# A four-stage transformer kernel on one core: the halves of the expert weights move in front of a weight split, and a norm's statistics move behind a residual add

## The chip, the core and the metric

The kernel runs on one core of a Trainium2 chip. The metric is the device time of one execution in microseconds (us); lower is better. TensorE (PE in the profile) multiplies matrices, with its weight loads as PEld; VectorE (DVE), ScalarE (ACT) and GpSimd (POOL) work on vectors, and SyncE (SP) issues the transfers. Each engine runs its own instruction list in the order in which it is written, and engines wait for each other by semaphores.

## The reference

Two transformer layers work on `x` (16 sequences of 64 tokens, 256 channels, float32). Each adds a gated cross attention and a gated feed-forward part. The part that matters here is the first layer's feed-forward, a mixture of 16 experts:

```python
probs = softmax(flat @ gate_w.T)
routing_weights, selected = top_k(probs, 4)
routing_weights = routing_weights / routing_weights.sum(-1)
comb = sum(one_hot(selected, 16) * routing_weights[..., None], axis=1)
for e in range(16):
    out_e = (silu(flat @ Wg[e]) * (flat @ Wu[e])) @ Wd[e]
    mixed = mixed + comb[:, e:e + 1] * out_e
shared = (silu(flat @ sWg) * (flat @ sWu)) @ sWd
return mixed + shared * sigmoid(flat @ shared_gate_w)
```

`flat` is the layer norm of `x`. Every expert is computed for every token, and the combined weight `comb` of token and expert scales its hidden values.

## The kernel before, in words

The 1024 tokens are worked on in four groups of 256 (`GROUPS`, two tiles of 128 rows each). There are four phases: A (cross attention of layer one), B (its experts), C (cross attention of layer two) and D (its feed-forward). Each phase runs over the four groups. The order of the work is written out by hand, once for each engine, in functions `pe_*`, `act_*`, `dve_*`, `pool_*` and `sp_*`; the last group of A and group 0 of B are interleaved in a merged stage (`pe_AB`, `act_AB`, `dve_AB`), and groups 1 to 3 of B are `pe_B`, `act_B`, `dve_B`. POOL has no merged function: it runs `pool_A` for all groups and then `pool_B` for all groups.

Float32 matmuls are made exact enough by splitting each operand into two halves: the upper half is a rounded copy (ACT, `nc.scalar.copy`), the lower half is what is left of it (a subtraction on DVE or POOL). `mm3` (L312) then multiplies upper by upper, upper by lower and lower by upper. So "halves" below always means such a pair.

One group of B, with k running over the 8 pairs of experts and the shared expert (`EC` = 8):

- `pe_B_gate_up` k makes gate and up of a pair in PSUM; ACT takes the tanh (`act_B_tanh`, L1090), DVE multiplies (`dve_B_gated`, L1169 and L1173), which gives h2.
- The router's logits become the combined weights on DVE. `pe_B_comb` (L971) turns them around with two transposes into 17 rows, `act_B_comb` (L1100) makes their upper half and `dve_B_comb` (L1229) their lower half.
- `pe_B_spread` k (L982) is one matmul with a selection matrix that spreads the two weights of a pair over the 128 hidden rows. The first one waits for both halves of the combined weights.
- `dve_B_weighted` k (L1179) multiplies h2 by the spread weights to h3; `act_B_upper` (L1105) and the loop of `pool_B` (L1304) make its halves, and `pe_B_down` k multiplies them with the down weights and sums over k in PSUM. It waits for both halves.
- Beside this, phase C's weights are prepared: `pe_B_join` r, for r from 0 to 3, multiplies two weight blocks into one PSUM bank (L644 for r of 0 and 1), `act_B_join` (L1117) and `dve_B_join` (L1185) make the halves of the product. Join r + 1 writes the same bank and so waits for the DVE's lower half of join r.

The order of PE in a group of B is: logits, gate/up 0, 1, 2, join 0, the transposes of the combined weights, gate/up 3, spread 0, spread 1, join 1, gate/up 4, down 0, and on. In the merged stage it is: gate/up 3, attention values, the transposes, gate/up 4, spread 0, spread 1, attention output (`pe_A_out`, L378 and at its end L382), down 0, spread 2, gate/up 5. Gate/up 5 writes the bank of the attention output and waits for the DVE's residual add (`dve_A_add`, L606).

The norm for the next group's `x` has three steps on three places: `front_stats` on DVE (L241, L245, L247) gives the variance, `front_pool` on POOL (L262) takes it to the power of -0.5, `front_norm` on DVE (L253) applies it; `front_pe` (L283) turns the result around for the matmuls much later in the group. On POOL the second step stands at the head of each group of B, and the change does not touch it:

```python
        def pool_B(pool, g):
            front_pool(pool, 5 + g)
            for k in range(EC + 1):
                n = rows_B(k)
                pool.wait_ge(*Bp["h_hi"].at(g, k + 1))
```

At the very start PE issues matmuls that only keep it going (`keep_warm`, L631).

Of the kernel before, what the change touches and what calls it, by code (L numbers as in the profile page):

```python
# [85 lines left out]
def build(nc, a):  # L86
    ctx = ExitStack()
    with ctx:
# [149 lines left out]
        def front_stats(dve, f, g):  # L238

            for t in range(TILES):  # L240
                nc.vector.bn_stats(stats[:, t, :], x[:, g * TILES + t, :]).then_inc(*front["stat"].up())  # L241
            for t in range(TILES):
                dve.wait_ge(*front["stat"].at(f, t + 1))
                dve.sem_inc(waited, 1)
                nc.vector.bn_aggr(mv[:, t, :], stats[:, t, :]).then_inc(*front["stat"].up())  # L245
            dve.wait_ge(*front["stat"].at(f, 4))
            nc.vector.tensor_scalar(ve, mv[:, :, 1], 1e-5, None, ALU.add).then_inc(*front["var_ready"].up())  # L247

        def front_norm(dve, f, g):

            dve.wait_ge(*front["rstd_ready"].at(f, 1))
            for t in range(TILES):
                nc.vector.tensor_scalar(xn[:, t, :], x[:, g * TILES + t, :], mv[:, t, 0:1], rstd[:, t:t + 1],  # L253
                                        ALU.subtract, ALU.mult).then_inc(*front["xn_ready"].up())
# [37 lines left out]
        def front_upper(act, f, to, hi=xT_hi):  # L292
            act.wait_ge(*front["xT_done"].at(f, 1))
            nc.scalar.copy(split_tokens(hi), ps[:, to, :]).then_inc(*front["hi_ready"].up())
# [620 lines left out]
        def rows_B(k):  # L915
            return P if k < EC else F
# [7 lines left out]
        def spread_of(k):  # L924
            return ps[:, (5, 2)[k % 2], 0:TG]

        def gate_B(g, k):
            bank = (6, 5, 4, 1, 0, 3, 1, 4, 3)[k] if g == 0 else (3, 4, 1)[k % 3]
            return ps[:, bank, 0:TG]
# [8 lines left out]
        def combT_B(g):  # L938
            return ps[0:E + 1, 6, TG:2 * TG]
# [145 lines left out]
        def act_B_tanh(act, g, k):  # L1085
            act.wait_ge(*Bp["gu_done"].at(g, k + 1))
            if k >= 3:
                act.wait_ge(*Bp["h1"].at(g, k - 2))
            n = rows_B(k)
            nc.scalar.activation(th[k % 3][0:n], gate_B(g, k)[0:n], ACT.Tanh,  # L1090
                                 scale=0.5).then_inc(*Bp["tanh_ready"].up())

        def act_B_router(act, g):
            act.wait_ge(*Bp["shifted"].at(g, 1))
            nc.scalar.activation(ex, ex, ACT.Exp).then_inc(*Bp["exp_ready"].up())
            nc.scalar.activation(sgate, lgs[:, :, E], ACT.Tanh, scale=0.5).then_inc(*Bp["gate_ready"].up())

        def act_B_comb(act, g):
            act.wait_ge(*Bp["combT_done"].at(g, 1))
            nc.scalar.copy(combT_hi, combT_B(g)).then_inc(*Bp["combT_hi"].up())  # L1100

        def act_B_upper(act, g, k):
            act.wait_ge(*Bp["h3"].at(g, k + 1))
            n = rows_B(k)
            nc.scalar.copy(h_hi[k % 3][0:n], h3[k % 3][0:n]).then_inc(*Bp["h_hi"].up())  # L1105

        def join_of(g, r):
            return (ps[:, 0, :] if g else joined[:, r]).rearrange("p (h n) -> p h n", h=2)

        def act_B_join(act, g, r):  # L1110
            if g:
                act.wait_ge(*Bp["join_done"].at(g, r + 1))
            elif r == 0:
                act.wait_ge(*A["x_done"].at(GROUPS, 0))
                act.wait_ge(joined_dve, 2)
            w = JOIN[r][0][:, bass.ds(g * HG + 2 * (r % 2), 2), :]
            nc.scalar.copy(w, join_of(g, r)).then_inc(*Bp["join_hi"].up())  # L1117
# [29 lines left out]
        def act_B(act, g):  # L1147
            act_B_tanh(act, g, 0)
            act_B_router(act, g)
            act_B_tanh(act, g, 1)  # L1150
            act_B_tanh(act, g, 2)
            act_B_join(act, g, 0)
            act_B_comb(act, g)
            act_B_upper(act, g, 0)
            for k in range(3, EC + 1):
                act_B_tanh(act, g, k)
                act_B_upper(act, g, k - 2)
                if k in (3, 5):
                    act_B_join(act, g, k // 2)
            front_upper(act, 5 + g, 0)  # L1160
            act_B_upper(act, g, EC - 1)
            act_B_upper(act, g, EC)
            act_B_join(act, g, 3)

        def dve_B_gated(dve, g, k):

            n = rows_B(k)
            dve.wait_ge(*Bp["tanh_ready"].at(g, k + 1))
            nc.vector.scalar_tensor_tensor(out=h1[k % 3][0:n], in0=th[k % 3][0:n], scalar=1.0,  # L1169
                                           in1=gate_B(g, k)[0:n], op0=ALU.add,  # L1170
                                           op1=ALU.mult).then_inc(*Bp["h1"].up())
            dve.wait_ge(*Bp["h1"].at(g, k + 1))
            nc.vector.tensor_tensor(h2[k % 3][0:n], h1[k % 3][0:n], up_B(g, k), ALU.mult).then_inc(*Bp["h2"].up())  # L1173

        def dve_B_weighted(dve, g, k):
            n = rows_B(k)
            dve.wait_ge(*Bp["h2"].at(g, k + 1))
            dve.wait_ge(*Bp["bc_done"].at(g, k + 1))
            nc.vector.tensor_tensor(h3[k % 3][0:n], h2[k % 3][0:n], spread_of(k)[0:n],  # L1179
                                    ALU.mult).then_inc(*Bp["h3"].up())  # L1180

        def dve_B_join(dve, g, r):
            dve.wait_ge(*Bp["join_hi"].at(g, r + 1))
            hi, lo = (w[:, bass.ds(g * HG + 2 * (r % 2), 2), :] for w in JOIN[r])
            nc.vector.tensor_tensor(lo, join_of(g, r),  # L1185
                                    hi.bitcast(F32), ALU.subtract).then_inc(*Bp["join_lo"].up())
# [40 lines left out]
        def dve_B_comb(dve, g):  # L1227
            dve.wait_ge(*Bp["combT_hi"].at(g, 1))
            nc.vector.tensor_tensor(combT_lo, combT_B(g), combT_hi.bitcast(F32),  # L1229
                                    ALU.subtract).then_inc(*Bp["combT_lo"].up())  # L1230
# [9 lines left out]
        def dve_AB(dve):  # L1240
            a, g = GROUPS - 1, 0
            dve_A_top(dve, a, 0)
            dve_A_top(dve, a, 1)
            dve_B_logits(dve, g)
            dve_A_lower(dve, a - 1)
            dve_A_sum(dve, a, 0)
            dve_A_sum(dve, a, 1)
            dve_B_choice(dve, g)
            dve_A_add(dve, a - 1)
            dve_B_weights(dve, g)  # L1250
            dve_B_gated(dve, g, 0)
            dve_B_gated(dve, g, 1)
            dve_B_gated(dve, g, 2)
            front_stats(dve, 5, 1)
            dve_A_lower(dve, a)
            dve_B_comb(dve, g)
            dve_B_weighted(dve, g, 0)
            dve_B_gated(dve, g, 3)
            dve_B_weighted(dve, g, 1)
            dve_B_gated(dve, g, 4)  # L1260
            dve_A_add(dve, a)
            front_norm(dve, 5, 1)
            for k in range(5, EC):
                dve_B_weighted(dve, g, k - 3)
                dve_B_gated(dve, g, k)
                dve_B_join(dve, g, k - 5)
            dve_B_weighted(dve, g, EC - 3)
            dve_B_gated(dve, g, EC)
            dve_B_weighted(dve, g, EC - 2)
            front_lower(dve, 5, 0)  # L1270
            dve_B_weighted(dve, g, EC - 1)
            dve_B_weighted(dve, g, EC)
            dve_B_join(dve, g, 3)
            dve_B_add(dve, g)

        def dve_B(dve, g):
            front_stats(dve, 5 + g, after(g))
            dve_B_logits(dve, g)
            dve_B_choice(dve, g)
            dve_B_weights(dve, g)  # L1280
            dve_B_gated(dve, g, 0)
            dve_B_gated(dve, g, 1)
            dve_B_gated(dve, g, 2)
            dve_B_join(dve, g, 0)
            dve_B_comb(dve, g)
            dve_B_weighted(dve, g, 0)
            front_norm(dve, 5 + g, after(g))
            for k in range(3, EC + 1):
                dve_B_weighted(dve, g, k - 2)
                dve_B_gated(dve, g, k)  # L1290
                if k in (3, 5):
                    dve_B_join(dve, g, k // 2)
            dve_B_weighted(dve, g, EC - 1)
            front_lower(dve, 5 + g, 0)
            dve_B_weighted(dve, g, EC)
            dve_B_join(dve, g, 3)
            dve_B_add(dve, g)
# [831 lines left out]
```

## Time and profile before

| | us |
|---|---|
| median of 3 runs | 404.07 |
| lowest, highest | 403.46, 405.74 |
| the profiled execution | 404.01 |
| its span on the core | 402.2 |
| PE busy | 374.7 (93%) |
| DVE busy | 312.0 (78%) |
| ACT busy | 194.0 (48%) |
| POOL busy | 168.9 (42%) |

The span runs from the first to the last instruction; what the profiled execution took beyond it (404.01 less 402.2) lies around it. Matmuls overlap, so a row of a matmul lasts longer than the distance to the next one: 0.28 us against about 0.12 us for 256 columns. Starts are therefore the better measure on PE. Experts and join work lie between 80 us and 191 us of the span: the merged stage up to 110 us, then groups 1, 2 and 3 of 27 us each.

### The profile page before, as it was taken

How to read it: one execution, taken by the hardware profiler on the slowest of the kernel's cores; microseconds unless marked ns; L12 is line 12 of the kernel's file. 1: busy time of each engine (PE TensorE's matmuls, PEld its weight loads, DVE VectorE, ACT ScalarE, POOL GpSimd, SP SyncE). 2: the span in 40 equal slices, each digit the busy share in tenths (PEclk: the TensorE clock that was granted, in tenths of full speed). 3: DMA queues.
4: the chain of work that ended last, by engine and by line, in shares of the span. 5: the costliest groups of instructions: out<-in, count | busy, mean ns of one | idle time of the engine just before them, and what ended most of it. 6: DMA issues, size and time to landing. Idle time of an engine off the chain costs nothing.

```text
span 402.2 us, 8995 instructions
## 1 busy us (share of the span) xinstructions
PE 374.7 (93%) x3586; PEld 351.7 (87%) x3594; DVE 312.0 (78%) x710; ACT 194.0 (48%) x401; POOL 168.9 (42%) x207
## 2 busy tenths in 40 slices
PE   0989999998999999999999999999999999999996
PEld 0777879887899999999999898999989999999996
DVE  3888878697786786775588988898899799965553
ACT  3577677742523333243356635554653556233332
POOL 4246646342303313123255545457424853632332
PEclk9999999999999999999999999999999999999999
DMA  7902102120000300300200010020001000000000
GB/s 219 337 13 78 57 30 80 34 102 2 0 2 0 133 2 1 132 0 10 75 0 2 6 63 2 2 67 3 2 0 56 3 0 2 2 10 19 27 28 27
DMA packets 7166, 16.33 MB, mean 41 GB/s; under 512 B 1218, under 2 KB 4803, under 8 KB 6740
## 3 DMA queue, kind: packets, MB, share of 16 engines
q1 hardware_dynamic: 7124, 15.75, 11.5%
q8 instruction: 28, 0.46, 0.5%
q14 instruction: 14, 0.11, 0.1%
HBM read 14.70 MB, written 1.05 MB: 39 GB/s over the span
## 4 chain that ended last, share of the span: by engine, by line
PE 60%; DVE 24%; ACT 8%; issue 4%; POOL 2%; DMA 1%; DVEq 0%
PE ps L312 37%; PE ps L1385 7%; DVE work L1656 4%; PE ps L414 2%; PE ps L378 2%; ACT work L1522 2%; DVE work L1173 2%; DVE work L1169 1%; ACT work L1500 1%; PE ps L1406 1%; DMA stage<-in_wA 1%; POOL workr L1304 1%; PE ps L982 1%; DVE workr L1613 1%; PE ps L425 1%
## 5 line engine op out<-in xcount | busy, mean ns | idle before, releaser
L1725 POOL TENSOR_SCALAR work<-work,lut_step,lut 128x344 f32<-128x344 int32 (+1 forms) x60 | 42.2, 715 | 53.6 <-DVE work L1641 52.0
L312 PE MATMUL ps<-wB_hi,workr 128*128 128x256 f32 x224 | 50.8, 293 | 3.0 <-POOL workr L1304 1.8
L312 PE MATMUL ps<-xT_hi,wB_hi 128*128 128x256 f32 x176 | 51.1, 290 | 0.3 <-DVE x L606 0.3
L312 PE MATMUL ps<-xT_lo,wB_hi 128*128 128x256 f32 x176 | 49.7, 282 | 0.0
L312 PE MATMUL ps<-xT_hi,wB_lo 128*128 128x256 f32 x176 | 49.7, 282 | 0.0
L1304 POOL TENSOR_TENSOR workr<-work,workr 128x256 fp32r<-128x256 f32 (+1 forms) x36 | 22.9, 636 | 62.3 <-ACT workr L1105 62.2
L312 PE MATMUL ps<-wN_hi,shared_r 128*128 128x256 f32 x256 | 47.8, 281 | 0.0
L1656 DVE COPY_PREDICATED work<-work 128x1376 f32<-128x1376 int32 (+5 forms) x36 | 42.1, 1168 | 2.2
L312 PEld LDWEIGHTS ps<-wB_hi,workr 128*128 128x128 f32 x224 | 38.2, 189 | 6.0 <-issue 3.3
L312 PEld LDWEIGHTS ps<-wN_hi,shared_r 128*128 128x128 f32 x256 | 40.2, 188 | 0.4 <-DVE shared_r L1618 0.3
L312 PE MATMUL ps<-xT_hi,wM_hi 128*128 128x256 f32 x128 | 36.6, 286 | 2.3 <-ACT work L1481 2.3
L312 PE MATMUL ps<-wN_lo,shared_r 128*128 128x256 f32 x128 | 35.6, 278 | 0.0
L312 PE MATMUL ps<-xT_lo,wM_hi 128*128 128x256 f32 x128 | 35.5, 277 | 0.0
L312 PE MATMUL ps<-xT_hi,wM_lo 128*128 128x256 f32 x128 | 35.5, 277 | 0.0
L312 PEld LDWEIGHTS ps<-xT_hi,wB_hi 128*128 128x128 f32 x176 | 33.5, 190 | 1.0 <-DVE x L606 0.5
L1090 ACT ACTIVATE work<-ps 128x256 f32<-128x256 f32 (+1 forms) x36 | 13.8, 384 | 41.7 <-PE ps L312 41.6
L312 PEld LDWEIGHTS ps<-xT_lo,wB_hi 128*128 128x128 f32 x176 | 33.5, 191 | 0.0
L312 PEld LDWEIGHTS ps<-xT_hi,wB_lo 128*128 128x128 f32 x176 | 33.5, 191 | 0.0
L1897 POOL TENSOR_TENSOR workr<-work,workr 128x256 fp32r<-128x256 f32 x24 | 19.5, 813 | 30.4 <-ACT workr L1844 30.2
L312 PE MATMUL ps<-wB_lo,workr 128*128 128x256 f32 x112 | 31.5, 281 | 0.0
L1385 PEld LDWEIGHTS ps<-stage,work 128*128 128x128 f32 x256 | 31.1, 192 | 0.4
L1385 PE MATMUL ps<-stage,work 128*128 128x64 f32 x256 | 30.3, 272 | 0.5
(220 smaller groups left out, 1072.7 us busy)
## 6 DMA issues: line engine op xcount, KB each, us to landing
stage<-in_wC SPq DMA_DIRECT2D x3, 1280.0 KB, 5.6
stage<-in_wB SPq DMA_DIRECT2D x4, 768.0 KB, 4.3
stage<-in_idx SPq DMA_DIRECT2D x4, 536.0 KB, 3.4
work<-in_wC SPq DMA_DIRECT2D x2, 640.0 KB, 7.7
stage<-in_wA SPq DMA_DIRECT2D x2, 512.0 KB, 5.6
out<-x SPq DMA_DIRECT2D x8, 128.0 KB, 1.8
x<-in_x SPq DMA_DIRECT2D x2, 256.0 KB, 4.6
x<-in_x SPq DMA_DIRECT2D x1, 512.0 KB, 9.7
```

The source lines that it names most:

```text
L312: last = nc.tensor.matmul(out, l, r, start=start and i == 0, stop=stop and i == 2)
L378: nc.tensor.matmul(ps[:, to, t * D:(t + 1) * D], l[:, c, tok], r[:, c, :], start=t == 0 and c == 0 and i == 0, stop=False, skip_group_chec ...
L414: last = nc.tensor.matmul(ps[:, p, k * S:(k + 1) * S], qx[r, k].rearrange("p h n -> p (h n)"), kT[r, k], start=k == 0, stop=False, skip_gr ...
L425: last = nc.tensor.matmul(o[:, :, lo:hi], ident_A, bc_last(neg_maxA[:, t, first:first + 8], hi - lo), start=False, stop=True, skip_group_c ...
L1090: nc.scalar.activation(th[k % 3][0:n], gate_B(g, k)[0:n], ACT.Tanh, scale=0.5).then_inc(*Bp["tanh_ready"].up())
L1173: nc.vector.tensor_tensor(h2[k % 3][0:n], h1[k % 3][0:n], up_B(g, k), ALU.mult).then_inc(*Bp["h2"].up())
L1304: nc.gpsimd.tensor_tensor(h_lo[k % 3][0:n], h3[k % 3][0:n], h_hi[k % 3][0:n].bitcast(F32), ALU.subtract).then_inc(*Bp["h_lo"].up())
L1385: last = nc.tensor.matmul(ps[:, 3 + s, k * S:(k + 1) * S], qt[:, 2 * s + jj, b].rearrange("p h n -> p (h n)"), ctx_g[:, b * S:(b + 1) * S] ...
L1522: nc.scalar.activation(lev[:, j, 0:n], bits[:, 0, 0:n], ACT.Identity, scale=lut_step[:, j:j + 1], bias=lut[:, 2 * j:2 * j + 1]).then_inc(* ...
L1656: nc.vector.copy_predicated(left, m, right).then_inc(*C["chosen"].up())
L1725: nc.gpsimd.tensor_scalar(lev[:, j, 0:n], bits[:, 0, 0:n], lut_step[:, j:j + 1], lut[:, 2 * j:2 * j + 1], ALU.mult, ALU.add).then_inc(*C[" ...
L1897: nc.gpsimd.tensor_tensor(fh_lo[i][0:n], fh3[k % 3][0:n], fh_hi[i][0:n].bitcast(F32), ALU.subtract).then_inc(*Dp["h_lo"].up())
```

## The change

In groups 1 to 3 of phase B the halves of the combined weights come before the halves of join 0, on ACT and on DVE. In the merged stage the DVE's statistics of the next norm go from in front of the lower halves of the attention output and of the combined weights to behind the residual add, and applying the norm goes from behind the add into the first round of the loop, behind join 0. ACT in the merged stage, PE and POOL keep their order.

```diff
 def act_B(act, g):
             act_B_router(act, g)
             act_B_tanh(act, g, 1)
             act_B_tanh(act, g, 2)
+            act_B_comb(act, g)
             act_B_join(act, g, 0)
-            act_B_comb(act, g)
             act_B_upper(act, g, 0)
 def dve_AB(dve):
             dve_B_gated(dve, g, 2)
-            front_stats(dve, 5, 1)
             dve_A_lower(dve, a)
             dve_B_comb(dve, g)
             dve_B_weighted(dve, g, 0)
             dve_B_gated(dve, g, 3)
             dve_B_weighted(dve, g, 1)
             dve_B_gated(dve, g, 4)
             dve_A_add(dve, a)
-            front_norm(dve, 5, 1)
+            front_stats(dve, 5, 1)
             for k in range(5, EC):
                 dve_B_weighted(dve, g, k - 3)
                 dve_B_gated(dve, g, k)
                 dve_B_join(dve, g, k - 5)
+                if k == 5:
+                    front_norm(dve, 5, 1)
 def dve_B(dve, g):
             dve_B_gated(dve, g, 2)
+            dve_B_comb(dve, g)
             dve_B_join(dve, g, 0)
-            dve_B_comb(dve, g)
             dve_B_weighted(dve, g, 0)
```

The DVE in the merged stage, before. The rows begin with the second half of gated 2; `L598` is the lower half of the attention output, `L1229` that of the combined weights, `L606` the residual add.

```order
L1173 TENSOR_TENSOR work<-work,ps 128x256
L241 BN_STATS stats<-x 128x6 x2
L245 BN_AGGR mv<-stats 128x2 x2
L247 TENSOR_SCALAR ve<-mv 128x2
L598 TENSOR_TENSOR workAr<-ps,workAr 128x2x4x64
L1229 TENSOR_TENSOR workr<-ps,workr 17x256
L1179 TENSOR_TENSOR work<-work,ps 128x256
```

And the same engine with the change, from `L598` on:

```order
L598 TENSOR_TENSOR workAr<-ps,workAr 128x2x4x64
L1229 TENSOR_TENSOR workr<-ps,workr 17x256
L1179 TENSOR_TENSOR work<-work,ps 128x256
L1169 SCALAR_TENSOR_TENSOR work<-work,ps 128x256
L1173 TENSOR_TENSOR work<-work,ps 128x256
L1179 TENSOR_TENSOR work<-work,ps 128x256
L1169 SCALAR_TENSOR_TENSOR work<-work,ps 128x256
L1173 TENSOR_TENSOR work<-work,ps 128x256
L606 SCALAR_TENSOR_TENSOR x<-ps,tg,x 128x512
L241 BN_STATS stats<-x 128x6 x2
L245 BN_AGGR mv<-stats 128x2 x2
L247 TENSOR_SCALAR ve<-mv 128x2
```

Five instructions of statistics now follow the add instead of preceding the two lower halves; nine instructions in front of them (two of weighting, four of gating, two lower halves, the add) moved ahead.

The DVE in groups 1 to 3, as one piece of the difference (join 0's lower half is `L1185`):

```order
 L1173 TENSOR_TENSOR work<-work,ps 128x256
+L1229 TENSOR_TENSOR workr<-ps,workr 17x256
 L1185 TENSOR_TENSOR wM_lo<-ps,wM_hi 128x512
-L1229 TENSOR_TENSOR workr<-ps,workr 17x256
 L1179 TENSOR_TENSOR work<-work,ps 128x256
```

The small subtraction passes the large one; the same happens to the two copies on ACT.

## Rows read from the trace of the kernel before

**Rows 1.** The page: TensorE's granted clock over the span in 40 slices.

```profile
PEclk9999999999999999999999999999999999999999
```

**Rows 2.** Who waited for whom: in total, times, longest, in us.

```profile
PE ps L982 <- DVE workr L1229: 3.0, 4, 1.2
...
PE ps L312 <- POOL workr L1304: 2.3, 8, 0.7
```

**Rows 3.** Timeline, merged stage: start, us, engine, line, operation, [idle before].

```profile
90.27 0.59 ACT L571 CAST workAr<-ps 128x512 fp32r<-128x512 f32 x1 [1.03 <-PE ps L528]
...
90.67 0.75 DVE L241 BATCH_NORM_STATS2 stats<-x 128x6 f32<-128x256 f32 x2
...
91.70 0.28 PE L312 MATMUL ps<-xT_hi,wB_lo 128*128 128x256 f32 x1
91.78 0.17 DVE L247 TENSOR_SCALAR ve<-mv 128x2 f32<-128x2 f32 x1
91.86 0.69 DVE L598 TENSOR_TENSOR workAr<-ps,workAr 128x512 fp32r<-128x512 f32 x1
92.03 0.70 POOL L262 TENSOR_TENSOR rstd<-ve,expo 128x2 f32<-128x2 f32 x1 [5.79 <-DVE ve L247]
92.57 0.41 DVE L1229 TENSOR_TENSOR workr<-ps,workr 17x256 fp32r<-17x256 f32 x1
93.13 0.47 PE L982 MATMUL ps<-workr 128*128 128x256 f32 x2 [1.15 <-DVE workr L1229]
```

**Rows 4.** Timeline, merged stage, from the halves of h3 to weighted 2.

```profile
94.54 0.64 POOL L1304 TENSOR_TENSOR workr<-work,workr 128x256 fp32r<-128x256 f32 x1 [1.81 <-ACT workr L1105]
...
94.86 0.40 PE L382 MATMUL ps<-workAr 128*128 128x512 f32 x1
...
95.33 0.36 PE L312 MATMUL ps<-wB_hi,workr 128*128 128x256 f32 x1
...
95.85 0.74 DVE L606 SCALAR_TENSOR_TENSOR x<-ps,tg,x 128x512 f32<-128x512 f32 x1
...
96.51 0.72 DVE L253 TENSOR_SCALAR xn<-x,mv,rstd 128x256 f32<-128x256 f32 x2
96.65 0.39 PE L312 MATMUL ps<-xT_hi,wB_hi 128*128 128x256 f32 x1 [0.26 <-DVE x L606]
...
97.15 0.41 DVE L1179 TENSOR_TENSOR work<-work,ps 128x256 f32<-128x256 f32 x1
```

**Rows 5.** Timeline, merged stage, rounds 5 and 6 of the DVE, and down 5.

```profile
98.80 0.42 DVE L1169 SCALAR_TENSOR_TENSOR work<-work,ps 128x256 f32<-128x256 f32 x1 [1.24 <-ACT work L1090]
...
101.06 0.42 DVE L1169 SCALAR_TENSOR_TENSOR work<-work,ps 128x256 f32<-128x256 f32 x1 [0.40 <-ACT work L1090]
...
106.47 0.36 PE L312 MATMUL ps<-wB_hi,workr 128*128 128x256 f32 x1 [0.69 <-POOL workr L1304]
```

**Rows 6.** Timeline, group 2 of the experts, from the transposes to join 1.

```profile
143.68 0.38 PE L971 MATMUL ps<-const,work 128*17 128x128 f32 x2
...
143.88 0.59 ACT L1117 CAST wM_hi<-ps 128x512 fp32r<-128x512 f32 x1 [0.51 <-PE ps L644]
...
144.36 0.36 ACT L1100 CAST workr<-ps 17x256 fp32r<-17x256 f32 x1
...
144.84 0.68 DVE L1185 TENSOR_TENSOR wM_lo<-ps,wM_hi 128x512 fp32r<-128x512 f32 x1
...
145.56 0.41 DVE L1229 TENSOR_TENSOR workr<-ps,workr 17x256 fp32r<-17x256 f32 x1
146.12 0.47 PE L982 MATMUL ps<-workr 128*128 128x256 f32 x2 [0.63 <-DVE workr L1229]
146.43 1.05 PE L644 MATMUL ps<-stage 128*128 128x128 f32 x8
```

**Rows 7.** Timeline of PE at the very start, after its first idle time.

```profile
9.38 2.47 PE L631 MATMUL ps<-shared_r 128*128 128x512 f32 x5 [9.38 <-ACT shared_r L1978]
...
13.27 3.05 PE L312 MATMUL ps<-shared_r,workAr 128*128 128x512 f32 x12 [0.32 <-issue]
```

## The prediction

> **What bounds the kernel now.** The page first: PE is busy for 93% of the span and its granted clock stands in the highest digit in all 40 slices [rows 1]. So time is won or lost only where PE waits. The list of waits comes next [rows 2]. The halves of the combined weights hold PE four times for 3.0 us together: the first spread matmul (L982) waits for the DVE's lower half (L1229). That is the wait that the change is after: 1.15 us in the merged stage [rows 3], 0.63 us in group 2 [rows 6], and the same in groups 1 and 3 (3.0 less 1.15 leaves 1.85 for three). The second line, down matmuls that wait for POOL's lower half of h3 (L1304), is short now, 2.3 us in eight waits, but it is the place to watch. POOL must run the norm's power (L262) before its first L1304, and that power waits for the last of the statistics, which the change puts later. The timelines give the distances.
>
> **The merged stage, up to the spread.** Before, the DVE starts the statistics at 90.67, the lower half of the attention output (L598) at 91.86, L1229 at 92.57; spread 0 starts at 93.13, which is 0.56 after L1229 [rows 3]. Without the statistics L598 may start when ACT's upper half ends, 90.27 + 0.59 = 90.86, plus about 0.05: 90.91. L1229 follows 0.71 later, as now (92.57 - 91.86): 91.62. Spread 0 follows 0.56 later: 92.18. PE is free by about 91.82 (its last matmul of gate/up 4 starts at 91.70 [rows 3]), so it still waits a little. Gain at spread 0: **0.95 us**. The attention output behind it starts as much earlier; its last matmul (L382) would run from 93.91 to 94.31 instead of from 94.86 to 95.26 [rows 4].
>
> **The merged stage, down 0.** Now the other side. The DVE behind spread 0 is dense, so the residual add (L606) goes from 95.85 [rows 4] to 94.90. The next DVE instruction starts 0.66 behind its start (96.51 - 95.85 [rows 4]), so the statistics start at 95.56. Their last instruction starts 1.11 after the first (91.78 - 90.67) and takes 0.17 [rows 3]: it ends at 96.84 instead of at 91.95. POOL's power starts 0.25 after the start of that instruction (92.03 - 91.78) and takes 0.70 [rows 3], from 96.92 to 97.62. Only then may POOL make the lower half of h3 of pair 0, which it does now at 94.54. PE's down 0 starts 0.79 behind that (95.33 - 94.54 [rows 4]): at **98.41 instead of 95.33, 3.08 us later**. PE has nothing to do from 94.31 to 98.41, since spread 2 and gate/up 5 are queued behind down 0. This is no deadlock: the add needs spread 0 and 1 and the attention output, all ahead of down 0. Part of it comes back at gate/up 5: it starts 1.32 after down 0 now, held by the add (0.26 idle [rows 4]), which will long be done. Six matmuls and a spread at 0.12 us and the slower first step behind a wait make it 0.90; the first step of gate/up 5 is short then too, another 0.10. So from there PE is 98.41 + 0.90 - 0.10 - 96.65 = **2.56 us late**.
>
> That GpSimd cannot let the later subtraction pass the waiting power is not shown by any row here. The Trainium skill, "Perfetto Trace Analysis", in the section on the Tensor Engine Instruction, says that ACT, DVE and GpSimd are strict first-in, first-out and only PE reorders a little. By that rule the sum is the one I make; without it, it would be the last rival below.
>
> **The moved instructions themselves.** The statistics lie on the DVE while PE stands anyway, and weighted 2 cannot start before spread 2. They cost nothing more. Applying the norm takes 0.64 (97.15 - 96.51 [rows 4]) and now stands in front of weighted 3. The DVE's idle time there is 0.40 in round 6 [rows 5], so 0.24 is not covered; it passes from round to round through the join copies on ACT and the join's lower halves, and reaches down 5, where PE waits for POOL already (0.69 at 106.47 [rows 5]). I take 0.2. Bounds: 0, if the rounds absorb it, and 0.64. The merged stage sums to 2.56 + 0.2 = **2.8 us lost**.
>
> **Groups 1 to 3.** In group 2 the transposes end at 143.68 + 0.38 = 144.06, so ACT's upper half may start at 144.10 instead of 144.36 and end at 144.46; the join copy follows and ends by 145.05. The DVE is free for L1229 at 144.84, where it now starts the join's lower half (L1185). Spread 0 then starts at 144.84 + 0.56 = 145.40 instead of 146.12: 0.72 gained. But join 1 needs L1185, now second: it starts at about 145.18, takes 0.68, and PE follows 0.15 after its end (146.12 against the end of L1229 at 145.97): 146.01. Join 1 starts at 146.43 now [rows 6]. So of 0.72 only 0.42 is left, and a second slow first step takes about 0.05: **0.37 a group, 1.1 for three**. Here a wait takes the place of the one removed, a shorter one. Bounds: 0 and 0.72 a group. Everything behind it (weighting, POOL's halves) starts 0.7 earlier and holds nobody. The later phases have no clock of their own: they shift.
>
> **Sum.** Against the profiled execution of 404.01 us: + 2.8 - 1.1 = + 1.7, so **405.7 us**. The median of the runs is 404.07, 0.06 above it, which is within the reading. A measurement of this kernel can tell about 0.5%, 2.0 us, from no change; 1.7 is 0.4%. So the most likely answer is a small loss that cannot be told from nothing, between 405.0 and 406.4 by its own bounds.
>
> **Rivals.**
>
> *The clock falls (slower).* Nowhere in the run before does PE stand longer than 1.15 us [rows 2, 3] except at the start, for 9.38 us. With the change it stands for 4.1 us. What a long stand does, the start shows: the first matmuls of 512 columns take 2.47 / 5 = 0.49 us each, the later ones 3.05 / 12 = 0.25 [rows 7]; that is the lower of its two levels, 1.2 against 2.4 GHz, although the page's digits do not show it. It lasted no longer than from 9.38 to 13.27, of which about 3 us count. The same behind 98.41 would do in 3 us what full speed does in 1.5: 1.5 us more, **407.2 us**. For it: the stand is 3.6 times the longest now. Against it: it is less than half of that at the start, and whether such a length is enough no row says. The Trainium skill, "TensorE: Matmul & The Clock Gate", on why this matters for your kernels, warns that an idle gap between bursts of matmuls drops the clock to half; by that rule this rival would be the answer, and the sum 407.2, in some executions at least. Chance 0.25.
>
> *The join takes all (slower).* If join 1 cannot start before 146.43, because the two subtractions or the two copies in the new order end no earlier than before, groups 1 to 3 gain nothing: 404.01 + 2.8 = **406.8 us**. For it: the sum of the two on the DVE is the same, and only the gap before L1229 (145.56 against the end of L1185 at 145.52) and the wait for PE's spread could be saved. Against it: the DVE's lower half of the join moves by only 0.34, while spread, 0.31 of it, no longer stands between. It decides where L1185 would end 0.26 later than I take it. Chance 0.08.
>
> *POOL does not hold down 0 (faster).* If the power does not stand in front of L1304, or the statistics end in time, the merged stage keeps its 0.95: 404.01 - 0.95 - 1.1 = **402.0 us**. For it: the wait that is removed is real. Against it: the list of `pool_B`, unchanged, has the power at its head, and the variance is made behind the add. It needs the power to end before 93.6 (94.54 less 0.95), and the add alone starts at 94.9. Chance 0.04.
>
> **How the numbers follow.** My forecast has 0.63, the rivals 0.25, 0.08 and 0.04. The predicted time is the likeliest case's, 405.7. The range takes in its own bounds and the clock: from 404.5 (where the groups gain 0.72 each, and the norm costs little) to 407.3. Slower by over 0.5% means over 406.1: a fifth of the forecast's cases, nearly all of the clock's and of the join's, 0.13 + 0.24 + 0.07 = 0.44. Faster by over 0.5% means under 402.05: about 0.03. The rest, 0.53, is the same.
>
> **What the profile would show.** Right: L982 waits for L1229 for under 0.4 us in the merged stage and next to nothing in the groups; one wait of PE for L1304 of about 4 us at 94 to 98 us; POOL's power at about 96.9 with L1304 directly behind it; the DVE's statistics behind L606; short waits of L644 for L1185, 0.4 us each. The clock's rival shows in matmuls of 256 columns behind 98.4 us that start about 0.21 us apart instead of 0.12. The prediction is wrong if down 0 starts before 97 us, if the groups from logits to logits do not shrink from 27.0 us, or if a wait appears in the rounds of the merged stage that is longer than 1 us.

## The result and the profile after

| | before | with the change |
|---|---|---|
| median of 4 runs, us | 403.77 | 408.36 |
| lowest, highest | 403.46, 405.74 | 407.53, 409.73 |
| the profiled execution | 404.01 | 407.53 |
| its span | 402.2 | 405.7 |

The ratio is 1.0101 with a 95% interval from 1.0072 to 1.0131: the change is 1.0% slower. The prediction of 405.7 and its range up to 407.3 were too low. Ratios and intervals, here and below, leave out executions that took over 1.5% longer than the fastest of their kernel.

The granted clock of the page and the first lines of PE's waits, after (answering to [rows 1, 2]):

```profile
PEclk9999999998999999999999999999999999999999
```

```profile
PE ps L312 <- POOL workr L1305: 6.5, 9, 4.1
...
PE ps L644 <- DVE wM_lo L1185: 0.5, 3, 0.2
...
PE ps L982 <- DVE workr L1229: 0.2, 1, 0.2
```

The wait at the spread fell from 3.0 to 0.2 us. (The change moved some lines: L1304 is L1305 now.) In its place stand others: one wait of 4.1 us for POOL's lower half, and three short ones of join 1 for the join's lower half. And one slice of the clock is no longer full. Below, a "stand" is a time in which TensorE has nothing that it may start.

The merged stage on the timeline, after (answering to [rows 3, 4]):

```profile
91.43 0.41 DVE L1229 TENSOR_TENSOR workr<-ps,workr 17x256 fp32r<-17x256 f32 x1
...
91.99 0.47 PE L982 MATMUL ps<-workr 128*128 128x256 f32 x2 [0.19 <-DVE workr L1229]
...
93.71 0.40 PE L382 MATMUL ps<-workAr 128*128 128x512 f32 x1
...
94.70 0.74 DVE L606 SCALAR_TENSOR_TENSOR x<-ps,tg,x 128x512 f32<-128x512 f32 x1
95.36 0.74 DVE L241 BATCH_NORM_STATS2 stats<-x 128x6 f32<-128x256 f32 x2
...
96.47 0.17 DVE L247 TENSOR_SCALAR ve<-mv 128x2 f32<-128x2 f32 x1
96.72 0.70 POOL L262 TENSOR_TENSOR rstd<-ve,expo 128x2 f32<-128x2 f32 x1 [10.67 <-DVE ve L247]
97.39 1.23 POOL L1305 TENSOR_TENSOR workr<-work,workr 128x256 fp32r<-128x256 f32 x2
98.17 0.55 PE L312 MATMUL ps<-wB_hi,workr 128*128 128x256 f32 x1 [4.06 <-POOL workr L1305]
...
99.80 0.41 PE L312 MATMUL ps<-xT_hi,wB_hi 128*128 128x256 f32 x1
100.01 0.41 PE L312 MATMUL ps<-xT_lo,wB_hi 128*128 128x256 f32 x1
...
101.08 0.28 PE L312 MATMUL ps<-xT_hi,wB_hi 128*128 128x256 f32 x1
101.20 0.28 PE L312 MATMUL ps<-xT_lo,wB_hi 128*128 128x256 f32 x1
```

This execution started 0.2 us sooner than that of before (the residual add of A's third group is at 86.43 instead of 86.63), so 0.2 goes off every predicted time. Down 0 was to start at 98.41, less 0.2: 98.21. It starts at 98.17. POOL is idle for 10.67 us before the power, then the lower half follows at once. What was not in the likeliest case of the forecast, only in its first rival, is the distance of the matmuls behind it: 0.21 us at 99.80, 0.12 us again from 101.08 on. The stretches of 1 us show the granted clock (the column in front of the last two; the columns before it are the length, then the busy time and count of PE, PEld, DVE, ACT and POOL):

```profile
96.00:97.00 1.00, 0.00 (x0) 0.00 (x0) 0.54 (x4) 0.00 (x0) 0.28 (x1) 1.00 0.00 0
97.00:98.00 1.00, 0.00 (x0) 0.00 (x0) 0.00 (x0) 0.00 (x0) 1.00 (x3) 0.82 0.00 0
98.00:99.00 1.00, 0.83 (x4) 0.86 (x5) 0.00 (x0) 0.00 (x0) 0.62 (x2) 0.50 0.00 0
...
100.00:101.00 1.00, 1.00 (x7) 1.00 (x6) 0.42 (x1) 0.00 (x0) 0.00 (x0) 0.50 0.00 0
101.00:102.00 1.00, 1.00 (x10) 1.00 (x9) 0.00 (x0) 0.01 (x1) 0.00 (x0) 0.97 0.06 16
```

While PE stands, the clock goes from 2.4 to 1.2 GHz. 0.82 in the stretch from 97 to 98 means that it fell at about 97.64. It came back at about 101.06.

Two distances measure the parts without the starting difference: from the residual add of A's third group (L606) to the first output add of the experts (L1236), which spans the merged stage, and from one output add to the next, a group. Before:

```profile
86.63 0.74 DVE L606 SCALAR_TENSOR_TENSOR x<-ps,tg,x 128x512 f32<-128x512 f32 x1
...
110.33 0.88 DVE L1236 SCALAR_TENSOR_TENSOR x<-ps,tg,x 128x256 f32<-128x256 f32 x2 [0.58 <-PE ps L312]
...
191.37 0.88 DVE L1236 SCALAR_TENSOR_TENSOR x<-ps,tg,x 128x256 f32<-128x256 f32 x2 [0.51 <-PE ps L312]
```

After:

```profile
86.43 0.74 DVE L606 SCALAR_TENSOR_TENSOR x<-ps,tg,x 128x512 f32<-128x512 f32 x1
...
114.15 0.88 DVE L1236 SCALAR_TENSOR_TENSOR x<-ps,tg,x 128x256 f32<-128x256 f32 x2 [0.58 <-PE ps L312]
...
194.71 0.88 DVE L1236 SCALAR_TENSOR_TENSOR x<-ps,tg,x 128x256 f32<-128x256 f32 x2 [0.52 <-PE ps L312]
```

The merged stage grew from 23.70 to 27.72 us, by 4.02. The three groups shrank from 81.04 to 80.56, by 0.48. Together that is 3.54 us. The spans differ by 3.5 as well, but partly by chance: the change started 0.2 us sooner, and a stretch of phase C took 0.2 more (23.95 against 23.74 us between two residual adds; in the traces of all the kernels below it is 23.6 to 24.0, so this is not the change's). Otherwise the later phases only shifted.

Group 2 after, from the transposes to gate/up 4 (answering to [rows 6]):

```profile
147.34 0.38 PE L971 MATMUL ps<-const,work 128*17 128x128 f32 x2
...
148.18 0.42 DVE L1173 TENSOR_TENSOR work<-work,ps 128x256 f32<-128x256 f32 x1
...
148.63 0.41 DVE L1229 TENSOR_TENSOR workr<-ps,workr 17x256 fp32r<-17x256 f32 x1
...
149.07 0.69 DVE L1185 TENSOR_TENSOR wM_lo<-ps,wM_hi 128x512 fp32r<-128x512 f32 x1
149.19 0.47 PE L982 MATMUL ps<-workr 128*128 128x256 f32 x2
...
149.82 1.16 PE L644 MATMUL ps<-stage 128*128 128x128 f32 x8 [0.16 <-DVE wM_lo L1185]
...
150.73 0.36 PE L312 MATMUL ps<-xT_hi,wB_hi 128*128 128x256 f32 x1
```

Gate/up 4 of group 2 before, beside [rows 6]:

```profile
147.24 0.36 PE L312 MATMUL ps<-xT_hi,wB_hi 128*128 128x256 f32 x1
```

Counted from the transposes, spread 0 starts 1.85 us later instead of 2.44, join 1 2.48 instead of 2.75, gate/up 4 3.39 instead of 3.56. So of 0.59 gained at the spread 0.27 are left at the join and 0.17 behind it: DVE's L1185 comes second and holds the bank.

### The profile page after: what moved, and what is told of

The parts are those of the page before. It is cut to its first block, busy times and chain, and to the rows that moved or that the text cites. A ratio compares the mean times of both kernels' runs of the same rounds, so it can differ in the third digit from the quotient of the medians.

```text
span 405.7 us, 8995 instructions
## 1 busy us (share of the span) xinstructions
PE 376.9 (93%) x3586; PEld 353.5 (87%) x3594; DVE 312.1 (77%) x710; ACT 194.2 (48%) x401; POOL 168.8 (42%) x207
## 4 chain that ended last, share of the span: by engine, by line
PE 62%; DVE 21%; ACT 8%; issue 4%; POOL 3%; DMA 1%; DVEq 0%
PE ps L312 38%; PE ps L1386 7%; DVE work L1657 4%; PE ps L414 2%; PE ps L378 2%; ACT work L1523 2%; POOL workr L1305 1%; ACT work L1501 1%; PE ps L1407 1%; DVE work L1173 1%; PE ps L513 1%; DMA stage<-in_wA 1%; DVE workr L1614 1%; PE ps L283 1%; POOL workA L614 1%
## 5 line engine op out<-in xcount | busy, mean ns | idle before, releaser
L1305 POOL TENSOR_TENSOR workr<-work,workr 128x256 fp32r<-128x256 f32 (+1 forms) x36 | 22.9, 636 | 61.0 <-ACT workr L1105 61.0
L262 POOL TENSOR_TENSOR rstd<-ve,expo 128x2 f32<-128x2 f32 x16 | 12.4, 776 | 47.6 <-DVE ve L247 47.3
```

What stands on the lines that cost most here:

```text
L262: nc.gpsimd.tensor_tensor(rstd, ve, expo, ALU.pow).then_inc(*front["rstd_ready"].up())
L1305: nc.gpsimd.tensor_tensor(h_lo[k % 3][0:n], h3[k % 3][0:n], h_hi[k % 3][0:n].bitcast(F32), ALU.subtract).then_inc(*Bp["h_lo"].up())
```

## The experiments

All ratios are against the kernel before on the same chip, with the 95% interval in brackets. "Stretch" is the distance from the third residual add to the first output add: 23.70 before, 27.72 with the change. It is read from the one profiled execution of each kernel. The pieces of code show the head of the function and the lines around the edit; what lies between is left out. The kernel before was measured again beside each experiment, and its median differed from chip to chip (404.08 to 405.18 us), so times of experiments on different chips compare only roughly.

**GpSimd's power behind pair 1.** The suspected hold is taken away, all else is the change.

```diff
 def pool_B(pool, g):
-            front_pool(pool, 5 + g)
+            if g:
+                front_pool(pool, 5 + g)
             for k in range(EC + 1):
+                if g == 0 and k == 2:
+                    front_pool(pool, 5 + g)
```

> The change as it is, with one thing more: in group 0 of the experts GpSimd takes the norm's power behind the lower halves of pairs 0 and 1 instead of in front of them. Theory (the power in front of the lower half of pair 0 holds down 0, and the long stand then drops the clock): down 0 starts about 2.1 us behind spread 0 as in the kernel before, no wait of PE for GpSimd over 0.3 us near 94 us, no matmuls 0.21 us apart behind it; the time is before less 0.95 for the spread and less 0.5 for the groups (0.17 each in the trace of the change), plus at most 0.2 for the norm in the round: 402.4 to 402.8 when before is 403.8. Rival (the loss comes from the moved statistics and norm on VectorE themselves): the time stays above 406.

Measured: 402.52 us (402.19 to 402.55, 5 runs), ratio 0.9957 (0.9944 to 0.9969). The trace of POOL:

```profile
93.24 0.64 POOL L1308 TENSOR_TENSOR workr<-work,workr 128x256 fp32r<-128x256 f32 x1 [7.33 <-ACT workr L1105]
94.35 0.64 POOL L1308 TENSOR_TENSOR workr<-work,workr 128x256 fp32r<-128x256 f32 x1 [0.47 <-ACT workr L1105]
96.56 0.71 POOL L262 TENSOR_TENSOR rstd<-ve,expo 128x2 f32<-128x2 f32 x1 [1.57 <-DVE ve L247]
```

L1308 is the lower half here. It starts at 93.24 instead of 97.39, the stretch is 22.93 (86.29 to 109.22), 0.77 under before, and the clock stays full. One call moved on an engine that the change did not touch turns 1.0% slower into 0.4% faster. The theory holds, the rival falls.

**Each part alone.** First only the part in groups 1 to 3 (the moved lines of `act_B` and `dve_B`), then only the part in the merged stage (those of `dve_AB`).

> Only the part in groups 1 to 3, merged stage as before. Theory (join 1 now waits for the join's lower half, which comes second on VectorE): each group gains 0.17 us, together 0.5, no more: 403.3 when before is 403.8; the wait of the spread matmul in the groups is gone and one for the join's lower half of 0.16 us stands there. Rival (each group gains what the spread's wait was, 0.6): 401.9.

Measured: 404.82 us (402.92 to 407.28, 12 runs), ratio 1.0021 (1.0001 to 1.0041). The time did not come out, the mechanism did: the groups take 80.51 us together (before 81.04), 0.5 less, the stretch is 23.68 as before, and L644 waits three times for L1185. What covers it lies in another place. The profiled execution, 404.57, shows its clock in phase A:

```profile
26.00:28.00 2.00, 2.00 (x54) 1.84 (x51) 1.65 (x5) 1.81 (x2) 0.68 (x2) 0.89 0.03 8
28.00:30.00 2.00, 2.00 (x7) 1.52 (x6) 2.00 (x5) 0.00 (x0) 2.00 (x2) 0.50 0.01 4
30.00:32.00 2.00, 2.00 (x10) 1.77 (x9) 1.22 (x7) 0.64 (x1) 1.67 (x2) 0.76 0.00 0
```

The code there is the same in all kernels. The clock fell at about 27.6 us and came back by 31; the same fall, at about 27.8 us, is in one other trace below, and in none of the rest. Three of the twelve executions have a recorded mean clock of 0.999 or 1.0, and took 402.92, 403.10 and 404.80 us; the other nine have 0.990 to 0.996 and 404.57 or more. So the trace shows no loss in the groups, only the gain of 0.5, and the whole time cannot resolve it. The three executions with a full clock point the same way: their median, 403.10, is below the 404.04 of the executions of before beside it with 0.998 or more. Where the clock fell in the executions that have no trace is not known, and why a mean of 0.996 or less is met more often here (9 of 12) than in before (3 of 17) stays open.

> Only the part in the merged stage, groups 1 to 3 as before. Theory: it holds the whole loss: 2.6 us of stand, 0.2 us of the norm in the round and 1.3 to 2.5 us of half clock behind the stand: 408 to 409 when before is 403.8, with the stand of 4.1 us in front of down 0 and matmuls of 256 columns 0.21 us apart for about 3 us. Rival (the two parts need each other for the loss): under 406.

Measured: 408.0 us (407.48 to 408.53, 4 runs), ratio 1.0099 (1.0085 to 1.0114). The stretch is 27.69 us (86.50 to 114.19). The merged stage holds the whole loss.

**The clock kept up by filling.** TensorE gets something to do during its stand.

```diff
 def pe_AB(pe):
             pe.wait_ge(*A["x_done"].at(a, 0))
+            keep_warm(16, 7)
             pe_B_down(pe, g, 0)
```

> The change as it is, with 16 matmuls of 512 columns added on TensorE in front of down 0, into a bank that nothing uses then; they take about 3.5 us at full clock, less than the stand of 4.1 us. Theory (half clock behind the stand is a cost of its own): down 0 starts when it did with the change, but no slow matmuls follow, and the time falls by 1.3 to 2.7 us against the change: 405.7 to 406.3 when before is 403.8, which is what the sum without the clock gave. Rival (the slow matmuls cost nothing, since other engines bind there): the time stays at 408.

Measured: the profiled execution took 405.68 us, the median of 6 runs was 407.56 (405.68 to 408.71), ratio 1.0088 (1.0069 to 1.0106). The trace came out as expected, the median did not. I repeated it with 15 instead of 16:

> As e4 with 15 filling matmuls instead of 16, so that they end clear of the start of down 0. The trace of e4 had no slow matmul and 405.7, but its other executions ran to 408.7. Theory (half clock costs 1.3 us where a stand of 4 us precedes it, and the fill prevents it): in the trace no matmuls 0.21 us apart and 405.7 to 406; the stretch from the third add to the first output add is 26.4 us, against 27.7 with the change. Rival (the fill does not matter, and e4's trace was a lucky execution): 27.7 us again in that stretch.

Measured: 407.2 us (405.81 to 412.65, 10 runs), ratio 1.0055 (1.0019 to 1.0091). Its trace:

```profile
86.99 0.74 DVE L606 SCALAR_TENSOR_TENSOR x<-ps,tg,x 128x512 f32<-128x512 f32 x1
...
94.49 3.60 PE L631 MATMUL ps<-shared_r 128*128 128x512 f32 x15
98.72 0.36 PE L312 MATMUL ps<-wB_hi,workr 128*128 128x256 f32 x1 [0.62 <-POOL workr L1306]
98.91 0.28 PE L312 MATMUL ps<-wB_lo,workr 128*128 128x256 f32 x1
99.03 0.40 PE L312 MATMUL ps<-wB_hi,workr 128*128 128x256 f32 x2
...
99.62 0.28 PE L312 MATMUL ps<-xT_hi,wB_hi 128*128 128x256 f32 x1
...
100.33 0.28 PE L312 MATMUL ps<-xT_hi,wB_hi 128*128 128x256 f32 x1
```

And the seventh matmul of gate/up 5 before:

```profile
97.47 0.28 PE L312 MATMUL ps<-xT_hi,wB_hi 128*128 128x256 f32 x1
```

Behind the fill the matmuls are 0.12 us apart, and the stretch is 26.41 us in both traces, in the second as written down ahead (26.4), against 27.72. Down 0 starts 11.7 us behind the third add in both, as it does with the change (98.17 less 86.43), so the fill did not move it. Two rows in each trace confirm the amount: from down 0 to the seventh matmul of gate/up 5 it is 1.61 us here (98.72 to 100.33) and 2.91 with the change (98.17 to 101.08). So the half clock costs **1.3 us**. The stand costs 2.5: that matmul lies 13.34 us behind the third add here, 10.84 before (97.47 less 86.63). The whole times do not show the 1.3 us: the fill's medians are 0.9% and 0.6% above before, and beside the first of them the merged part alone had 408.0, only 0.4 more where 1.8 would be due (1.3 for the clock, 0.5 for the groups). Both kernels have executions over 2 us longer than their profiled one, and even with a recorded clock of 1.0 they differ (405.68, 406.24 and 407.46 in the first). No trace of the longer ones exists, so what they lose is open.

**How long a stand.** The statistics go to two earlier places, POOL keeps its order.

```diff
 def dve_AB(dve):
             dve_B_weighted(dve, g, 0)
             dve_B_gated(dve, g, 3)
             dve_B_weighted(dve, g, 1)
+            front_stats(dve, 5, 1)
             dve_B_gated(dve, g, 4)
             dve_A_add(dve, a)
-            front_stats(dve, 5, 1)
```

> The change, but in the merged stage the statistics stand behind weighted 1, before gated 4 and the add. GpSimd keeps its order. Theory: the variance is ready 1.2 us earlier, down 0 starts at 96.7 instead of 98.2, after a stand of 2.6 us instead of 4.1; the stage loses 1.1 against before, the norm 0.2, the groups give 0.5 back: 404.8 if the clock stays up, with matmuls of 256 columns 0.12 us apart behind the stand; 406 to 407.5 if a stand of 2.6 us is enough to drop it. Rival (the loss hangs on the order of VectorE around the add and not on GpSimd's power): no better than the change, 408.

Measured: 406.72 us (404.04 to 412.87, 10 runs), ratio 1.0024 (0.9993 to 1.0055). The stand is 2.62 us and the clock falls:

```profile
97.28 0.55 PE L312 MATMUL ps<-wB_hi,workr 128*128 128x256 f32 x1 [2.62 <-DVE x L606]
97.63 0.41 PE L312 MATMUL ps<-wB_lo,workr 128*128 128x256 f32 x1
...
98.91 0.41 PE L312 MATMUL ps<-xT_hi,wB_hi 128*128 128x256 f32 x1
99.12 0.41 PE L312 MATMUL ps<-xT_lo,wB_hi 128*128 128x256 f32 x1
```

The row names the add as releaser, but the add was started at 96.44 and is not waited for here; POOL's lower half, from 96.49, ends the wait (0.79 us from its start to down 0, as in [rows 4]). The stretch is 26.26 us, 1.46 less than with the change, and down 0 starts 1.46 sooner behind the third add: the half clock costs as much as there. Nine of the ten executions have a mean clock of 0.996 or less and 405.6 us or more; the one with 1.0 took 404.04, about 2.7 us less than the middle of the others. It has no trace. A full clock behind the stand would explain 1.3 of that; the rest is open, and executions of before beside it with 0.999 or 1.0 spread from 403.61 to 405.33.

> The change, with the statistics in the merged stage behind weighted 0, so that the variance is ready 2.3 us earlier; GpSimd's order as it is. Theory: TensorE's stand in front of down 0 is 1.5 us (4.1 with the change, 2.6 in e5, under 0.3 in before). In before a stand of 1.15 us left the clock up, in e5 one of 2.6 dropped it. If 1.5 leaves it up: matmuls 0.12 us apart behind it, gate/up 5 starts 0.1 to 0.2 us later than in before, and 403.8 in all when before is 404.0. If it drops it: 405.1, with matmuls 0.21 us apart. Rival (the drop in the change has nothing to do with the length of the stand): slow matmuls here too, as in the change.

Measured: 404.61 us (403.51 to 405.92, 10 runs), ratio 0.9983 (0.9955 to 1.0012). The stretch is 24.15 us. The stand is shorter and the clock stays up behind it:

```profile
97.26 0.36 PE L312 MATMUL ps<-wB_hi,workr 128*128 128x256 f32 x1 [1.48 <-POOL workr L1305]
97.46 0.28 PE L312 MATMUL ps<-wB_lo,workr 128*128 128x256 f32 x1
97.57 0.40 PE L312 MATMUL ps<-wB_hi,workr 128*128 128x256 f32 x2
```

The six executions with a recorded clock of 1.0 took 403.51 to 404.76, with a median of 403.86. Its profiled execution has the fall in phase A, from about 27.8 to 31.2 us, which has nothing to do with this place. The whole time cannot be told from before; that the stand matters is read from the matmul distances. Between stands of 1.48 us (up) and 2.62 us (down) the traces of this kernel leave it open.

**Join 1 behind gate/up 4.** On top of the first experiment, to test what eats the rest of the gain in the groups.

```diff
 def pe_B(pe, g):
             pe_B_spread(pe, g, 1)
-            pe_B_join(pe, g, 1)
             pe_B_gate_up(pe, g, 4)
+            pe_B_join(pe, g, 1)
             pe_B_down(pe, g, 0)
```

> As e1 (GpSimd's power behind pair 1), and in groups 1 to 3 TensorE takes join 1 behind gate/up 4 instead of in front of it. Theory (in the groups the rest of the gain is eaten by join 1's wait for its bank, held by the second subtraction): each group gets about 0.4 us more, from 26.85 to 26.4 us, together 1.2: 401.3 against 402.5 for e1; no wait of L644 for L1185. Rival (the groups are bound elsewhere by then, by the chain to down 0 or the later join copies): 402.3 to 402.6.

Measured: 401.51 us (400.82 to 401.77, 6 runs), ratio 0.9886 (0.9836 to 0.9937; the kernel before had a median of 405.18 beside it and spread widely, so the ratio flatters: the spans of the two traces, 399.9 against 402.2 us, differ by 0.6%). A group takes 26.42 us (109.54 to 135.96), as expected, and no wait of L644 for L1185 is left. Against 27.01 before that is 0.59, all that spread 0 had gained: the rest sat behind the join's bank.

**Where the norm stands.** Two versions on top of that; `front_norm` gets the tiles to work on as an argument.

```diff
 def dve_AB(dve):
                 dve_B_weighted(dve, g, k - 3)
                 dve_B_gated(dve, g, k)
                 dve_B_join(dve, g, k - 5)
-                if k == 5:
-                    front_norm(dve, 5, 1)
+                if k < 7:
+                    front_norm(dve, 5, 1, (k - 5,))
```

> As e6, and the two tiles of the norm are applied in rounds 5 and 6 of the merged stage, one each, instead of both in round 5. Theory (0.64 us of norm in one round overflows VectorE's idle 0.40 by 0.2 that reaches down 5; 0.32 in each of two does not): 0.2 us less from the add of the third to the first output add of the experts, 22.7 instead of 22.9 us in the trace, and 401.1 in all. Rival (the join's lower half was late for another reason): no difference in that stretch.

Measured: 402.12 us (400.99 to 408.75, 11 runs), ratio 0.9913 (0.9874 to 0.9952). The stretch is 22.95 us (87.00 to 109.95), as in the version before it (22.94): a miss. My reading was that halving the block did not help because each half still stood in front of a weighting, and the weighting feeds ACT's upper half. The next version tests it.

```diff
                 dve_B_weighted(dve, g, k - 3)
+                if k > 5:
+                    front_norm(dve, 5, 1, (k - 6,))
                 dve_B_gated(dve, g, k)
                 dve_B_join(dve, g, k - 5)
-                if k < 7:
-                    front_norm(dve, 5, 1, (k - 5,))
```

> As e7, but each tile of the norm stands between the weighting and the gating of rounds 6 and 7, where VectorE waits 0.40 us for the tanh, instead of behind the join's lower half and so in front of the next weighting. Theory (what the norm costs is that it delays the weighting behind it, and with it the upper half on ScalarE; in the gap for the tanh it delays nothing): the stretch from the third add to the first output add falls from 22.95 to 22.75 us; in all 0.2 us less than e6, 401.3. Rival (the 0.2 us is not the norm's): 22.9 to 23.0 again.

Measured: 401.57 us (400.89 to 405.08, 12 runs), ratio 0.9937 (0.9916 to 0.9958). The stretch is 22.73 us (86.33 to 109.06), as expected: the 0.2 us are gone. It is 0.97 under before, about what spread 0 had gained (0.94). Down 5 shows where the 0.2 had gone. Its wait for POOL, 0.69 in [rows 5], with the change, with join 1 later (and the same 0.86 with the split norm), and here:

```profile
110.28 0.36 PE L312 MATMUL ps<-wB_hi,workr 128*128 128x256 f32 x1 [0.86 <-POOL workr L1305]
```

```profile
105.67 0.36 PE L312 MATMUL ps<-wB_hi,workr 128*128 128x256 f32 x1 [0.86 <-POOL workr L1308]
```

```profile
105.19 0.36 PE L312 MATMUL ps<-wB_hi,workr 128*128 128x256 f32 x1 [0.70 <-POOL workr L1308]
```

This version also applies the norm one round later than the one before it, which no run separates from the place within the round. The medians of this version and of the one with join 1 later are alike, though on different chips; both are better than either kernel of this study.

## Why the prediction was wrong

*The spread, down 0, gate/up 5.* Right to within 0.06 us: spread 0 at 91.99 (92.18 less 0.2), the power at 96.72 (96.92 less 0.2), down 0 at 98.17, and a cost of 2.50 us where 2.56 was forecast. The step that carries the loss, POOL's power in front of its lower half, is shown by the first experiment: without it the loss is gone.

*The clock.* This is the step that failed. The forecast took the stand of 4.1 us as one that leaves the clock up, with a chance of 0.63, and gave the fall 0.25. Both traces, of the change and of its merged part alone, show the fall behind the stand, and all eight executions of these two kernels have a mean clock of 0.996 or less. The reasoning was that 4.1 is less than half of the stand at the start; nothing in the trace stood between 1.15 and 9.38, and "less than half" was no argument. The size was nearly right: 1.5 forecast, 1.3 measured by the fill. The warning of the Trainium skill, "TensorE: Matmul & The Clock Gate", on why this matters for your kernels, that an idle gap between bursts of matmuls drops the clock to half, is what this trace showed at a stand of 4.06 us.

*The groups.* The mechanism was right, the size was not: 0.37 a group forecast, 0.16 measured (0.48 / 3). The subtraction of the combined weights was put 0.33 us behind the multiplication in front of it on the DVE, and L1185 0.34 behind that, which are the distances of other rows; they are 0.45 (148.18 to 148.63) and 0.44 (148.63 to 149.07), and the same in the other groups. With that L1185 comes 0.23 later than forecast, counted from the transposes, and join 1 0.15 later. The slower first step of the join cost 0.10 instead of 0.05. For this term the rival in which the join takes all was slightly nearer than the forecast.

*The norm.* 0.2 forecast, and right, down to the place: 22.94 against 22.73 us in the last experiments is 0.2, and the wait at down 5 grew from 0.69 to 0.86. The merged stage lost 4.02, which is 2.50 for the stand, 1.3 for the clock and 0.2 for this. But it was not the overflow of VectorE's idle time by 0.24 as such, since splitting the norm over two rounds saved nothing; what the last experiment speaks for is that the norm stood ahead of the weighting.

*The sum.* 404.01 + 2.50 + 0.2 + 1.3 - 0.5 = 407.5, and the profiled execution took 407.53. So against the 405.7 of the forecast 1.3 were missing for the clock and 0.6 for the groups. The median, 408.36, is another 0.8 higher: two of the four executions, 409.03 and 409.73, have a mean clock of 0.992 instead of 0.995. A second fall like the one seen in phase A in other kernels would fit; with no trace of these executions it is not shown.

*The range.* Its top, 407.3, took the clock's fall together with the full gain of 1.1 in the groups. With the prediction's own 1.5 for the clock and the 0.48 that the groups gained, its sum is 407.8. And the 405.0 to 406.4 called the forecast's "own bounds" are narrower than the bounds given for its terms: 0 and 0.64 for the norm and 0 and 0.72 a group allow 404.4 to 407.2.

## What to carry to other kernels

When a producer is moved later on one engine, look at the lists of all engines that wait for it: here an untouched list had the consumer at its head, in front of work that TensorE needed. Price a new stand of TensorE twice, once as waiting and once as half clock behind it, unless the trace holds a stand of that length that left the clock up. And where a wait is removed by swapping two instructions, ask at once who waits for the one that is now second.

## What the runs showed of the hardware

- In the traces a stand of 1.48 us left TensorE's clock up, stands of 2.62 and 4.06 us took it from 2.4 to 1.2 GHz. It fell during the stand (at 97.64 in the change, at about 96.8 with the stand of 2.62) and came back 2.9 us after the first matmul behind it (98.17 to 101.06, and 97.28 to about 100.2). The matmuls of 256 columns in between were 0.21 us apart instead of 0.12, which cost 1.3 us.
- In the kernel with the stand of 2.62 us one execution in ten has a recorded clock of 1.0. It was about 2.7 us shorter than the middle of the others, more than the half clock explains, and it has no trace.
- In two traces, of different kernels, the clock also fell from about 27.6 to 31 us in phase A, where PE was idle for 0.85 us and then took about 2 us for 64 matmuls of 64 columns before the clock fell. The trace of before has the same rows there with a full clock. The two executions took 1.5 and 1.35 us over the median of those of their kernel with a clock of 0.999 or 1.0.
- On GpSimd a power of two columns that waited for its variance held back a subtraction that was ready: 97.39 us with the power in front of it, 93.24 in the first experiment with the power behind it.
- The recorded clock does not show the slow first matmuls of the program [rows 7]; their distance does.
